# Edge chunks of 128 instead of 125, a first product of 128 rows, and expert pieces of 112 and 117

## The reference

```
layer 0:  x = x + GatedGraph(norm(x), src, dst) + LinearAttention(norm(x))
          x = x + Experts(norm(x))            # 6 experts, all computed
layer 1:  xn = norm(x)
          hid = silu(edge_attr_8 @ fc_w0 / sqrt(8))        # per edge, 8 -> 64
          w   = hid @ fc_w1 / sqrt(64)                     # 64 -> 256
          mid = products of w, h[src] and edge_attr_4      # 8 x 64 per edge
          x = x + Linear(segment_sum(mid, dst)) + GalerkinAttention(xn)
          x = x + sum over 2 of 8 experts of  w2 (silu(w1 x) * (w3 x))   # inner features 682
```

## Time and profile before

| | before |
|---|---|
| runs, us | 4054.32, 4057.44, 4058.73 (median 4057.44) |
| span of the profiled execution | 4057.3 us |
| its own time around the span | not given; the span lies 0.14 us below the median |
| TensorE busy (matmul) | 3711.8 us, 91% of the span |
| VectorE, ScalarE, GpSimd busy | 2525.8, 1533.3, 758.0 us |
| mean granted TensorE clock | 0.959 of full speed |

### The profile page before, as it was taken

How to read it: one execution, slowest core, us unless ns; L and a number is a source line. 1 busy time by engine, 2 the same in 40 slices (tenths; PEclk the granted TensorE clock), 3 DMA queues, 4 the chain that set the end, 5 groups by cost and what they waited for, 6 DMA issues and landing times. The chain is left out here.

```text
span 4057.3 us, 61050 instructions
## 1 busy us (share of the span) xinstructions
PE 3711.8 (91%) x18981; PEld 3087.0 (76%) x18981; DVE 2525.8 (62%) x5060; ACT 1533.3 (38%) x3578; POOL 758.0 (19%) x614
## 2 busy tenths in 40 slices
PE   5996879999999999999998799787999999779996
PEld 2554459989899899898997688655888888758884
DVE  7774755555555555555554555544777777577775
ACT  0363211121211211212112544334888886135553
POOL 0000000000000000000000200003888885012221
PEclk9997989999999999999999899898999999779998
DMA  1364112222222222222221211012333332411113
GB/s 41 64 102 87 48 50 78 87 67 85 76 79 86 74 80 87 67 85 76 79 85 40 66 30 31 13 41 61 93 93 93 94 93 68 177 44 35 38 35 116
DMA packets 297743, 288.61 MB, mean 71 GB/s; under 512 B 101485, under 2 KB 272847, under 8 KB 296806
## 3 DMA queue, kind: packets, MB, share of 16 engines
q1 hardware_dynamic: 233867, 208.29, 17.8%
q0 software_dynamic: 56576, 66.41, 6.4%
q10 hardware_dynamic: 7002, 10.15, 0.7%
HBM read 241.89 MB, written 42.47 MB: 70 GB/s over the span
## 5 line engine op out<-in xcount | busy, mean ns | idle before, releaser
L974 PE MATMUL bank<-a_wide,parts 125*128 125x448 f32 x4200 | 871.5, 367 | 0.1
L974 PEld LDWEIGHTS bank<-a_wide,parts 125*128 125x128 f32 x4200 | 785.7, 188 | 77.2 <-issue 10.1
L2205 POOL DMA_INDIRECT rows<-h_dram,src_t x400 | 493.5, 1234 | 124.1 <-DVE prod L2394 87.3
L2321 ACT ACTIVATE hot<-eq,ea 125x80 f32<-125x80 f32 x1600 | 413.2, 350 | 0.0
L949 POOL TENSOR_TENSOR nf_g<-nf,nf_g 128x896 fp32r<-128x896 f32 x42 | 94.5, 2249 | 1525.4 <-ACT nf_g L1112 1525.4
L1024 DVE CAST a_wide<-a_cols 125x2240 fp32r<-125x2240 bf16 x210 | 274.5, 1324 | 156.5 <-PE bank L974 141.0
L983 PE MATMUL bank<-nf_g,whh 128*128 128x448 f32 x1512 | 339.6, 369 | 0.0
L983 PE MATMUL bank<-msg,wc 128*128 128x448 f32 x1512 | 338.9, 368 | 0.0
L2247 PEld LDWEIGHTS bank<-prod,hot 125*80 125x80 f32 x2400 | 294.6, 150 | 54.1 <-issue 0.7
L2247 PE MATMUL bank<-prod,hot 125*80 125x128 f32 x2400 | 327.9, 273 | 0.0
L1117 ACT ACTIVATE msg<-bank 128x448 fp32r<-128x448 f32 x84 | 41.1, 542 | 702.6 <-PE bank L974 702.6
(11 more groups left out here) (431 smaller groups left out, 5894.4 us busy)
## 6 DMA issues: line engine op xcount, KB each, us to landing
a_cols<-a_dram SPq DMA_DIRECT2D x210, 546.9 KB
a_dram<-a_cols SPq DMA_DIRECT2D x15, 1250.0 KB, 10.9
w<-in_w SPq DMA_DIRECT2D x4, 2728.0 KB
deg_bc<-deg_dram SPq DMA_DIRECT2D x42, 224.0 KB, 6.1
gate_bc<-gate_dram SPq DMA_DIRECT2D x42, 224.0 KB, 3.2
rows<-h_dram,src_t POOLq DMA_INDIRECT x400, 4.2
w<-y_rows SPq DMA_DIRECT2D x12, 512.0 KB, 10.1
w<-in_w SPq DMA_DIRECT2D x5, 1024.0 KB
```

What stands on the lines that cost most here:

```text
L974: ins = nc.tensor.matmul(p_msg[f][:, 0:GW], parts[0:SPB, m, c * HB + k, f * 128:(f + 1) * 128], a_wide[u % 2][0:SPB, k, :], start=(c == 0 ...
L2205: nc.gpsimd.indirect_dma_start(out=rows[n % ITC][:, :], out_offset=None, in_=h_dram, in_offset=bass.IndirectOffsetOnAxis(ap=src_t[:, n:n + ...
L2321: ins = nc.scalar.activation(hot[:, q % 2, j, m, :], eq[:, q % 2, j, :], ACT.Copy, scale=ea4[:, q * UC + j, m:m + 1])
```

## The change

Edge chunks hold 128 edges; there are 392 of them, so 50176 places, of which the last 176 are filled: source 0, edge features 0, and a target outside every tile and window (the chunk table used for ranges repeats the last real target). A unit has 512 edges, and there are 98. `ea8` and `fw0` get 128 partitions, cleared once by POOL; rows 0 to 23 are filled as before, and the first product runs over all 128 rows. SP waits for the clearing before its first load of edge features, VectorE before it writes `fw0`. The experts' inner features are cut into four pieces of 112 and two of 117. The loads of a 117-piece are split into 112 rows and 5 rows, so there are eight loads of `w2` in place of six. ScalarE copies 112 partitions of the first four transposes, VectorE both of the last two with one instruction of 117 partitions.

```diff
-EC, NCH = 125, 400
+E, EC = 50000, 128
+NCH = 392
-HCH = [(k * 128, min(128, HID1 - k * 128)) for k in range((HID1 + 127) // 128)]
+LONG, SHORT = (4, 112), (2, 117)
+HCH = [(k * LONG[1], LONG[1]) for k in range(LONG[0])] + [(LONG[0] * LONG[1] + k * SHORT[1], SHORT[1]) for k in range(SHORT[0])]
...
-        ea8 = sb(ctx, "ea8", [24, 2, UE], F32R)
+        ea8 = sb(ctx, "ea8", [128, 2, UE], F32R)
-        fw0 = sb(ctx, "fw0", [24, 128], F32R)
+        fw0 = sb(ctx, "fw0", [128, 128], F32R)
...
+                sp.wait_ge(rest_zero, START + 2)
-                        sp.dma_start(ea8[:, b, :].bitcast(F32), ea8_dram[:, q * UE:(q + 1) * UE]).then_inc(ea_in[b], 16)
+                        sp.dma_start(ea8[0:24, b, :].bitcast(F32), ea8_dram[:, q * UE:(q + 1) * UE]).then_inc(ea_in[b], 16)
...
+                nc.gpsimd.memset(fw0[:, :].bitcast(F32), 0.0).then_inc(rest_zero, 1)
+                nc.gpsimd.memset(ea8[:, :, :].bitcast(F32), 0.0).then_inc(rest_zero, 1)
                 nc.gpsimd.memset(acc[:, :, :], 0.0).then_inc(acc_zero, 1)
...
+                dve.wait_ge(rest_zero, START + 2)
-                nc.vector.tensor_tensor(fw0[:, :], fw0_raw[:, :], fw0_high[:, :], ALU.subtract).then_inc(w_split, 1)
+                nc.vector.tensor_tensor(fw0[0:24, :], fw0_raw[:, :], fw0_high[:, :], ALU.subtract).then_inc(w_split, 1)
...
     for h, (o, sz) in enumerate(HCH):
-        sp.dma_start(w2[0:sz, :, h, :], A["w2_1"][:, o:o + sz, :].rearrange("e p n -> p e n")).then_inc(w_in, 16)
+        even = sz // 16 * 16
+        for a, b in ((0, even), (even, sz)):
+            if b > a:
+                sp.dma_start(w2[a:b, :, h, :], A["w2_1"][:, o + a:o + b, :].rearrange("e p n -> p e n")).then_inc(w_in, 16)
...
-                    nc.scalar.activation(g_t[:, 0:IN_0, :], p_g[0][:, 0:IN_0 * 128].rearrange("p (h c) -> p h c", c=128), ACT.Copy)\
+                    nc.scalar.activation(g_t[0:LONG[1], 0:IN_0, :], p_g[0][0:LONG[1], 0:IN_0 * 128].rearrange("p (h c) -> p h c", c=128), ACT.Copy)\
...
-                    nc.vector.tensor_copy(g_t[:, IN_0:NH - 1, :], p_g[1][:, 0:(NH - 1 - IN_0) * 128].rearrange("p (h c) -> p h c", c=128))
-                    at_h = (NH - 1 - IN_0) * 128
-                    nc.vector.tensor_copy(g_t[0:sz, NH - 1, :], p_g[1][0:sz, at_h:at_h + 128]).then_inc(gt_done, 1)
+                    nc.vector.tensor_copy(g_t[0:SHORT[1], IN_0:NH, :], p_g[1][0:SHORT[1], 0:SHORT[0] * 128].rearrange("p (h c) -> p h c", c=128))\
+                      .then_inc(gt_done, 1)
```

More of the change, by code:

```diff
@@ L2121, in edge_convolution @@
     src_t, rel0, base_row, rounds_t, iota_w = tables
-    (w_in, w_split, silu_done, hid_high, scaled, acc_zero, tab, ea_in_a, ea_in_b, hid_mm, hid_done, w_mm, eq_done, hot_done, p_done, sum_mm, sum_copied, turned, added,
+    (w_in, w_split, silu_done, hid_high, scaled, rest_zero, acc_zero, tab, ea_in_a, ea_in_b, hid_mm, hid_done, w_mm, eq_done, hot_done, p_done, sum_mm, sum_copied, turned, added,
      u_mm, mix_mm, t_done, b_done, x_done, stat_done, passed, *gathered) = sems(*("c_" + s for s in (
-         "w_in w_split silu hid_high scaled acc_zero tab ea_in_a ea_in_b hid_mm hid w_mm eq hot prod sum_mm sum_copied turned added "
+         "w_in w_split silu hid_high scaled rest_zero acc_zero tab ea_in_a ea_in_b hid_mm hid w_mm eq hot prod sum_mm sum_copied turned added "
          "u_mm mix_mm t b x stat passed").split()),
@@ L2458, in _ @@
                 aggregate(NT - 1)
-EXPERT_LOADS = 2 * KD + len(HCH)
+EXPERT_LOADS = 2 * KD + len(HCH) + SHORT[0]
 def load_experts(sp, A, w13, w2, w_in):
@@ L2751, in expert_swiglu @@
     G0 = 2 * UW - HID1
-    IN_0 = 4
+    IN_0 = LONG[0]
     groups = [(t, min(t + 2, NT)) for t in range(0, NT, 2)]
@@ L2953, in turned @@
                     dve.wait_ge(y_mm, START + n)
-                    o, sz = HCH[-1]
-                    nc.vector.tensor_copy(g_t[:, IN_0:NH - 1, :], p_g[1][:, 0:(NH - 1 - IN_0) * 128].rearrange("p (h c) -> p h c", c=128))
-                    at_h = (NH - 1 - IN_0) * 128
-                    nc.vector.tensor_copy(g_t[0:sz, NH - 1, :], p_g[1][0:sz, at_h:at_h + 128]).then_inc(gt_done, 1)
+                    nc.vector.tensor_copy(g_t[0:SHORT[1], IN_0:NH, :], p_g[1][0:SHORT[1], 0:SHORT[0] * 128].rearrange("p (h c) -> p h c", c=128))\
+                      .then_inc(gt_done, 1)
                 def output(n):
@@ L2999, in layouts @@
     z[:N] = np.asarray(i["node_vec1"])[:, 0]
+    src_e, dst_e, dst_n = np.zeros(NCH * EC, np.int32), np.full(NCH * EC, int(NOWHERE) // KT, np.int32), np.full(NCH * EC, dst[-1], np.int32)
+    src_e[:E], dst_e[:E], dst_n[:E] = src, dst, dst
+    ea4, ea8 = np.zeros((NCH * EC, 4), np.float32), np.zeros((NCH * EC, 8), np.float32)
+    ea4[:E], ea8[:E] = i["edge_attr_4"], i["edge_attr_8"]
     pad8 = np.zeros((128, 8), np.float32)
@@ L3015, in layouts @@
         "x_rows": c(x.reshape(NT, RT, D).transpose(1, 0, 2)),
-        "src_t": c(src.reshape(NCH, EC).T),
-        "dst_t": c(dst.reshape(NCH, EC).T),
-        "dst_c": c(dst.reshape(NU, UE)),
+        "src_t": c(src_e.reshape(NCH, EC).T),
+        "dst_t": c(dst_e.reshape(NCH, EC).T),
+        "dst_c": c(dst_n.reshape(NU, UE)),
         "wkv0": c(np.concatenate([i["L0_mix_wk"], i["L0_mix_wv"]], axis=1)),
@@ L3024, in layouts @@
         "z_rows": c(z.reshape(NT, RT).T),
-        "ea4": c(np.asarray(i["edge_attr_4"]).reshape(NCH, EC, 4).transpose(1, 0, 2)),
-        "ea8": c(np.asarray(i["edge_attr_8"]).T),
+        "ea4": c(ea4.reshape(NCH, EC, 4).transpose(1, 0, 2)),
+        "ea8": c(ea8.T),
         "wlin": np.concatenate([diag(i["L1_gnn_W_lin1_0"], i["L1_gnn_W_lin1_1"]),
```

## The result

The changed kernel takes 3987.77 us (median of four runs, 3982.65 to 3990.47) against 4057.76 (four runs, 4054.32 to 4058.73): the ratio is 0.9825, 95% interval 0.9811 to 0.9839. Forecast was 3983, range 3972 to 4003.

| stretch | before, us | after, us | gain | forecast |
|---|---|---|---|---|
| start to the first adjacency product | 45.97 | 44.48 | 1.5 | 0.6 |
| adjacency, first to last product | 274.68 | 269.04 | 5.6 | 5.6 |
| from there to the edge stage's first instruction | 2470.20 | 2471.52 | -1.3 | 0 |
| edge stage: its start to the first one-hots | 15.02 | 13.86 | 1.2 | 2.3 |
| first one-hots to the last transposition | 625.44 | 581.41 | 44.0 | 46.6 |

What follows compares the result with a forecast made beforehand. TensorE was taken as the bound, POOL right behind or level. Setup 0.6, adjacency 5.6, edge-stage start 2.3, two fewer units 12.3, first product 34.3, experts 19.6 make 74.7; 4057.3 - 74.7 = 3983 us, range 3972 to 4003.

Steps and rivals of the forecast that it cites:

- What bounds the kernel: Edge and expert stages: TensorE is the bound, idling beside products of 24 and 42 rows because changing tiling mode drains it.
- Rival B: Edge stage and experts: height costs nothing, the gaps have another cause, such as semaphores; 4037 us, chance 0.04.
- D: Experts: pieces of 112 and 117 stall too, so the experts give nothing; 4003 us, chance 0.02.
- Adjacency and experts: Adjacency stage: 251 pairs instead of 256 save 5.6 us; expert stage: 0.35 us saved per block, 56 blocks, 19.6 us.
- Setup: Tables before the adjacency stage: 400 columns instead of 408 make VectorE's work shorter, 0.6 us (0 to 1.5).
- The first product: Edge stage: on 128 rows it costs 0.23 us, not 0.58; 0.35 saved per unit, x 98 = 34.3 us.
- the two units: Edge stage: two units fewer at 6.16 us each save 12.3 us.
- POOL: Edge stage: gathers of 128 rows take 0.97 us, 5.1 per unit, so POOL stays below the unit of 5.81.
- Rival A: Edge stage: 128-row gathers cost what 125-row ones do, POOL becomes the bound, unit 6.15; 4016 us, chance 0.07.
- Start of the edge stage: Before L2374: loads on 128 partitions land sooner, while POOL's new clearings take 1.2 us; gain 2.3 us (0 to 4).
- the 12.5 to 13 that I had named as a sign: Edge stage: L2374 starting 12.5 to 13 us after the stage's first instruction, not 15.0, would show the forecast right.
- Loads of the experts: SP's queue before the expert stage: eight loads instead of six cost nothing; 11 us if their cover were gone.

## Why the prediction was right, and where it was off

*What bounds the kernel: right.* The gaps beside 24 and 42 rows were TensorE's own, and the runs at 64 and 65 rows put the edge where the prediction's modes of up to 64 rows had it. Rival B is out (24 rows cost 28 us again), and so is D (72 rows are as good as 117).

*Adjacency and experts: right to a tenth* (5.6 and 19.6). *Setup* gave 1.5 instead of 0.6, and most of that is luck: VectorE's first conversion, which waits for a load, started at 4.97 us and not at 6.17, and from there to the first product only 0.3 us were gained. Two traces with chunks of 125 start the table of one-hots 0.8 us apart (at 9.4 and 10.2 us).

*The first product: right mechanism, size a little off.* A unit gained 0.34, not 0.35, and it is 96 units, not 98: the loop makes its product two units ahead, so the last two have none inside, and the two made before the loop lie where TensorE waits. 96 x 0.34 = 32.6 instead of 34.3. With 2 x 6.15 = 12.3 for the two units that is 44.9. The stage fell 0.9 short of it, and nearly all of that is the first unit, 8.28 us long against 7.77 before, where 0.34 less was counted; why it grew stays open.

*POOL: right outcome.* The gather of 128 rows costs what the experts' gather showed. But I priced its failure wrongly. Rival A kept the unit at 6.15 and still made the kernel faster; with chunks of 125 the measured unit is 6.51, since the gather that meets VectorE's split of the hidden features grew from 1.3 to 1.71 when its start shifted to just behind L2376. By that unit, A would have been 98 x (6.51 - 6.15) = 35 us above its 4016.

*Start of the edge stage: one term mis-sized.* The loads came sooner by 4.7 us, more than I assumed, and I had taken that VectorE would only stand behind the clearing through its wait before L2374. It stood behind it from its first copy, so six small instructions still followed it: 1.2 instead of 2.3, and the first one-hots 13.9 us after the stage's first instruction, outside the 12.5 to 13 that I had named as a sign.

*Loads of the experts: right.* SP's timeline, against the earlier trace rows:

```profile
3468.34 36.92 SPq L2480 DMA_DIRECT2D w<-in_w  x8
3505.31 0.56 SPq L2554 DMA_DIRECT2D xn_dram<-weight  x1
```

Eight issues took 36.92 us against 33.14, the store came 5.1 us later in its stage (53.9 for 48.8 after the stage's first instruction; the rest of it is the four loads before, 16.46 for 15.13), and no other engine waited for it. The remaining shortfall, 1.7 us, lies in stretches that the change doesn't touch; in the profiled kernels with the same code up to the edge stage, that stage starts anywhere from 2778.9 to 2792.8 us, so a term of a few us can only be read inside its stretch.

## What to carry to other kernels

Look for products whose contraction (the number of rows that a product sums over) has 64 rows or fewer among taller ones: padding to 65 or more, or cutting the pieces evenly, gave back 0.35 us for each passage down and up here. Before a stage's bound is made shorter, price the next engine by its interval when nothing holds it (here 1.51 us a gather, not its busy time), and change both in one step: one of these edits alone was a loss. Try gathers and loads with a number of partitions that 16 divides, even if the last rows are unused: here 128 for 125 took a gather from 1.21 to 0.95 us.

## What the runs showed of the hardware that I had not expected

The threshold is sharp: 64 rows pay in full, 65 nothing. A gather of 128 rows is shorter than one of 125 (0.95 against 1.21 us), and so is one that fetches three rows for nobody. A clearing of 11.04 us on POOL made a 0.37 us copy on VectorE last 3.80; in the other direction a gather that began 0.05 us behind a VectorE subtraction took 1.71 us for 1.21, in 89 units of 100, while gathers that began up to 0.04 us behind it were not held.
